# Linear attention on one core: outer products by pair of heads, the carry's sum on VectorE, half sums in the last turn

## The chip, the core and the metric

The kernel runs on one core of a Trainium2 chip. The metric is the device time of one execution in microseconds (us), the median of several. TensorE (PE) multiplies, VectorE (DVE), ScalarE (ACT) and GpSimd (POOL) work element by element, SyncE (SP) issues DMAs. Each engine takes its instructions in the order in which they are written, and waits on semaphores.

## What is computed

A block of 4 x 1024 tokens of width 128: an expert layer, then chunked linear attention with decay, then the same expert layer once more, each added to the tokens. Only the attention is touched here:

```python
def step(kv, xs):                       # 8 chunks of 128 tokens
    qi, ki, vi = xs                     # 4 batches, 16 heads of 8
    scores = einsum('bhid,bhjd->bhij', qi, ki) * mask
    o = einsum('bhij,bhjd->bhid', scores, vi)
    o = o + lam_q[:, :, None] * einsum('bhid,bhde->bhie', qi, kv)
    kv = lam_c[:, None, None] * kv + einsum('bhid,bhie->bhde', ki * lam_k[:, :, None], vi)
    return kv, o
# q, k, v = silu(x @ Wq), silu(x @ Wk), silu(x @ Wv), split into heads
# then a layer norm of o, times sigmoid(x @ Wg1 @ Wg2), @ Wo, added to x
```

## The kernel before

It has three stages: expert layer 0 (to about 147 us of the span), attention in eight turns, one per chunk of all four batches (147 to 307 us), then routing and expert layer 1. The attention kernel does not form the scores. For each token it forms the outer product of k and v of each head (8 x 8 numbers, 64 per head, 1024 per token and batch), multiplies these with a decay matrix over the 128 tokens of the chunk (a matmul per head: the running state at each token), multiplies by q, and sums over d. What comes from earlier chunks goes by a carry, a block-diagonal 128 x 128 matrix per batch.

In turn n, for pairs of heads h = 0 to 7:

- GpSimd forms the outer products (`outer_part`, line L301 through `outer_product`): one instruction makes 512 numbers of one batch and half of the heads; 8 instructions a turn. The four of the first half for turn n + 1 are at the end of turn n, the four of the second half at the start of turn n + 1 around the first half sum. For turn 0 VectorE makes the first half (`first_outer`).
- TensorE forms the state products of pair h (`state_product`, L1287) into bank h % 3. For h = 0 it waits until all four products of the first half are done, for h = 4 for the second half. Between the pairs it does the output product of turn n - 2, the transposes and projections (L1266) of turn n + 1, the gate product; after them the inter product (L1295, needs the carry), the carry product (L1304, needs kd and qdT of turn n + 1), the transposes of o_n (L1184) and the router's product (L1190).
- VectorE multiplies by q (`times_q`, L988, qS with four buffers) and sums over d (`sum_d`, L997, into o_in). For h = 0, 1, 2, 4, 5, 6 of turns 0 to 6, GpSimd first adds the two halves of qS (`half_sum`, L461), and the sum is over 256 numbers in place of 512. Between these stand the small steps of the layer norms, which end in `shift` (L759); `front` makes qdT (L978) behind the steps of pair 6; `join` (L1007), `gate` (L1016), the router's bias (L780) and the statistics (L719) stand at the turn's end and start.
- ScalarE copies xnT, does `age_carry` (L644, L645: the carry times its decay; the new part out of PSUM), then Silu of q, k and v in one instruction per batch (L603, in the first expert layer's end L613), tanh of the gate, and the norms (L544, L636).
- GpSimd also scales the keys (`decay_keys`, L432, kd), masks the new part of the carry and adds it (`update_carry`, L439 and L444), and in turns 0 to 3 fetches the first expert layer's results of the last three chunks back, three indirect DMAs a turn (`fetch_one`, L404), each chunk followed by an add (`add_back`, L411).

After turn 7 VectorE routes the tokens of the first five chunks (L818 to L906), GpSimd gathers them, and expert layer 1 starts.

The order on GpSimd is written out by hand in its `attention(n)`. `helped(n, h)` says which pairs get a half sum.

## Time and profile before

| | us |
|---|---|
| median of 3 runs | 452.91 |
| lowest, highest | 452.79, 458.83 |
| profiled execution: its time | 454.72 |
| profiled execution: its span, first to last instruction | 452.7 |
| mean granted TensorE clock of the profiled execution | 0.928 |

Busy shares of the span: PE 81%, DVE 65%, POOL 65%, ACT 43%. Half of the instructions of TensorE are weight loads, counted apart (PEld). The span is counted from the first instruction. "Idle before" is the time for which an engine stood still ahead of an instruction, with what ended that; L12 is line 12 of the kernel. A granted clock of 1.00 is the 2.4 GHz level. The records of instructions that follow one another closely overlap by up to some 0.1 us, so back to back a duration counts for a little less.

### The profile page before, as it was taken

How to read it: one execution, taken by the hardware profiler on the slowest of the kernel's cores; microseconds unless marked ns; L12 is line 12 of the kernel's file. 1: busy time of each engine (PE TensorE's matmuls, PEld its weight loads, DVE VectorE, ACT ScalarE, POOL GpSimd, SP SyncE). 2: the span in 40 equal slices, each digit the busy share in tenths (PEclk: the TensorE clock that was granted, in tenths of full speed). 3: DMA queues.
4: the chain of work that ended last, by engine and by line, in shares of the span. 5: the costliest groups of instructions: out<-in, count | busy, mean ns of one | idle time of the engine just before them, and what ended most of it. 6: DMA issues, size and time to landing. Idle time of an engine off the chain costs nothing.

```text
span 452.7 us, 10251 instructions
## 1 busy us (share of the span) xinstructions
PE 364.9 (81%) x2508; PEld 325.6 (72%) x2508; DVE 293.9 (65%) x996; ACT 195.9 (43%) x586; POOL 294.2 (65%) x306
## 2 busy tenths in 40 slices
PE   4966999999988977886859889852388999999930
PEld 4955988999977765765657767732387988999920
DVE  3594567444464886685949898897856677666510
ACT  2552663555545232435344745413065434555500
POOL 0006772763886699989787898910277777777771
PEclk9999999999999999696969999995669999999985
DMA  7736787787861000001010101101278855776510
GB/s 230 268 94 203 226 234 183 217 202 217 222 181 30 20 6 17 4 16 46 20 47 1 47 2 46 46 2 46 74 215 241 202 185 161 219 209 198 159 35 0
DMA packets 41303, 54.00 MB, mean 119 GB/s; under 512 B 6212, under 2 KB 25818, under 8 KB 40992
## 3 DMA queue, kind: packets, MB, share of 16 engines
q1 hardware_dynamic: 34496, 39.49, 27.8%
q0 software_dynamic: 6176, 13.26, 12.2%
q10 hardware_dynamic: 576, 0.62, 0.5%
q8 instruction: 23, 0.38, 0.3%
q14 instruction: 32, 0.26, 0.2%
HBM read 41.93 MB, written 12.32 MB: 120 GB/s over the span
## 4 chain that ended last, share of the span: by engine, by line
PE 48%; POOL 23%; DVE 11%; issue 10%; DMA 3%; DVEq 1%; ACT 1%; POOLq 1%; ACTq 0%
PE bank L1238 15%; PE bank L1228 15%; POOL outer_all L301 9%; PE bank L1287 5%; POOL rows L404 4%; POOL qS L461 4%; PE bank L1190 3%; PE bank L1184 2%; PE bank L1266 2%; PE bank L1220 2%; PE bank L1322 2%; POOL out_x L423 1%; DMA const_sb<-in_const 1%; DVE outer_all L895 1%; POOL rows L411 1%
## 5 line engine op out<-in xcount | busy, mean ns | idle before, releaser
L390 POOL DMA_INDIRECT ring<-rows_d,token_in x92 | 88.1, 957 | 98.2 <-DVE token_in L906 71.4
L1228 PE MATMUL bank<-slot_xT,w_ring 128*128 128x128 f32 x736 | 104.7, 285 | 5.3 <-DVE hT_b L946 4.4
L1228 PEld LDWEIGHTS bank<-slot_xT,w_ring 128*128 128x128 f32 x736 | 94.6, 199 | 8.5 <-DVE hT_b L946 6.2
L1287 PE MATMUL bank<-outer_all,decay_sb 128*128 128x256 f32 x256 | 69.5, 397 | 14.6 <-POOL outer_all L301 12.6
L946 DVE TENSOR_SCALAR hT_b<-bank,b_cur 128x128 f32<-128x128 f32 x184 | 55.9, 345 | 38.5 <-PE bank L1228 32.8
L1287 PEld LDWEIGHTS bank<-outer_all,decay_sb 128*128 128x128 f32 x256 | 48.5, 198 | 32.0 <-POOL outer_all L301 13.8
L1238 PE MATMUL bank<-w_sb,hT_a 128*128 x368 | 60.6, 288 | 3.7 <-issue 0.9
L301 POOL TENSOR_TENSOR outer_all<-qkv 128x512 f32<-128x512 f32 x60 | 62.6, 1069 | 1.5 <-ACT qkv L613 1.4
L575 ACT ACTIVATE hT_a<-bank,b_cur 128x128 f32<-128x128 f32 x184 | 57.5, 364 | 12.9 <-PE bank L1228 12.4
L1238 PE MATMUL bank<-w_sb,hT_b 128*128 x368 | 56.8, 277 | 0.0
L423 POOL DMA_INDIRECT out_x<-ring,token_out x46 | 46.7, 1014 | 14.0 <-issue 12.5
L1238 PEld LDWEIGHTS bank<-w_sb,hT_a 128*128 128x128 f32 x368 | 49.4, 195 | 8.8 <-issue 8.3
L997 DVE TENSOR_REDUCE o_in<-qS 128x64 f32<-128x256 f32 (+1 forms) x64 | 47.8, 758 | 12.1 <-POOL qS L461 11.7
L988 DVE TENSOR_TENSOR qS<-bank,qkv 128x512 f32<-128x512 f32 x64 | 43.9, 686 | 17.6 <-PE bank L1287 17.4
L568 ACT ACTIVATE b_cur<-b_t 128x4 f32 x92 | 18.8, 205 | 82.0 <-DVE hT_b L946 62.2
L1238 PEld LDWEIGHTS bank<-w_sb,hT_b 128*128 128x128 f32 x368 | 49.3, 195 | 0.0
L461 POOL TENSOR_TENSOR qS<-qS 128x256 f32<-128x256 f32 x42 | 30.5, 728 | 18.1 <-DVE qS L988 17.9
L404 POOL DMA_INDIRECT rows<-y_d,slot_of x32 | 30.7, 960 | 14.0 <-DMA y_d<-y_sb 6.9
L560 ACT ACTIVATE slot_xT<-bank 128x128 f32<-128x128 f32 x92 | 25.0, 272 | 19.0 <-PE bank L1220 15.4
L1220 PE MATMUL bank<-const_sb,ring 128*128 128x128 f32 x92 | 26.3, 286 | 5.3 <-DMA ring<-rows_d,token_in 2.7
L938 DVE TENSOR_TENSOR ring<-ring,b_sb 128x128 f32<-128x128 f32 x46 | 13.4, 292 | 21.4 <-issue 17.4
L719 DVE BATCH_NORM_STATS2 st<-rows 128x6 f32<-128x128 f32 x96 | 20.7, 279 | 8.8 <-DMA rows<-in_x 7.5
(130 smaller groups left out, 528.3 us busy)
## 6 DMA issues: line engine op xcount, KB each, us to landing
w_ring<-in_w1t SPq DMA_DIRECT2D x92, 256.0 KB
rows_d<-rows SPq DMA_DIRECT2D x8, 512.0 KB, 2.9
y_d<-y_sb SPq DMA_DIRECT2D x46, 64.0 KB
rows<-in_x SPq DMA_DIRECT2D x8, 256.0 KB, 7.5
w_sb<-in_w2t SPq DMA_DIRECT2D x1, 2048.0 KB, 8.6
rows_d<-rows SPq DMA_DIRECT2D x8, 256.0 KB, 2.8
ring<-rows_d,token_in POOLq DMA_INDIRECT x92
decay_sb<-in_decay SPq DMA_DIRECT2D x1, 1024.0 KB, 7.5
```

The source lines that it names most:

```text
L301: return eng.tensor_tensor(u_.rearrange("p (h d e) -> p h d e", d=HD, e=HD), k_.rearrange("p (h d) e -> p h d e", d=HD), v_, ALU.mult)
L390: pool.indirect_dma_start(n_in_ring(G) if layer_of(G) == 0 else in_ring(G), None, rows_d[u], bass.IndirectOffsetOnAxis(ap=token_in[u][:, j ...
L404: pool.indirect_dma_start(n_of(t), None, y_d[u], bass.IndirectOffsetOnAxis(ap=slot_of[u][:, t - UNIT[u].first:t - UNIT[u].first + 1], axis ...
L423: pool.indirect_dma_start(out, bass.IndirectOffsetOnAxis(ap=token_out[u - GROUPS][:, at:at + 1], axis=0), x_in_ring(G), None, bounds_check ...
L461: pool.tensor_tensor(v[:, :, 0], v[:, :, 0], v[:, :, 1], ALU.add).then_inc(halved, 1)
L575: last = nc.scalar.activation(hT_a[G % 2][:, f * P:(f + 1) * P], bank_a[:, f * P:(f + 1) * P], ACT.Relu, bias=b1_cur[G % 2][:, f:f + 1])
L946: last = nc.vector.tensor_scalar(hT_b[G % 2][:, f * P:(f + 1) * P], bank_b[:, f * P:(f + 1) * P], b1_cur[G % 2][:, 2 + f:3 + f], 0.0, ALU. ...
L988: nc.vector.tensor_tensor(qS[h % 4][:, :].rearrange("p (b a e) -> p b a e", b=BATCH, e=HD), bank[h % 3][:, :].rearrange("p (b a e) -> p b ...
L997: nc.vector.tensor_reduce(o_in[:, h * w:(h + 1) * w].rearrange("p (a e) -> p a e", e=HD), qS[h % 4][:, :].rearrange("p (a d e) -> p a e d" ...
L1228: last = mm(to[:, f * P:(f + 1) * P], w1_ring[G % W1_BUFS][:, (2 * half + f) * P:(2 * half + f + 1) * P], slot_xT[G % 2][:, :], start=True ...
L1238: last = mm(y_bank[l][:, 0:D], h[:, f % 2 * P:(f % 2 + 1) * P], w2_sb[:, bass.ds(expert[G] + f * D, D)], start=(f == 0), stop=(f == FB - 1))
L1287: last = mm(to, decay_sb[:, (2 * h + a) * P:(2 * h + a + 1) * P], u, start=True, stop=True)
```

## The change

- q, k and v have another layout in SBUF: q of all batches first, then k and v by head, then batch, then element. Silu becomes two instructions per batch, one for k and v (256 columns, written in runs of 8), one for q.
- One outer-product instruction makes one pair of heads for all four batches (512 numbers again), and all are GpSimd's, turn 0's too. State product h waits for h + 1 of them. In GpSimd's order five (pairs 0 to 4) stand at the end of the turn before, three (5 to 7) at the start of the turn. Pair 0's stands before half sum 6 in turns without an `add_back`.
- The carry is kept unmasked: VectorE computes carry_all = carry_all x decay + new part, straight from PSUM, at the turn's start before `times_q(0)`; GpSimd masks it into carry with one instruction, once the last inter product has read it. `age_carry` goes from ScalarE.
- The 12 fetches are spread as 2, 3, 3, 2, 2 over turns 0 to 4, and `add_back` stands after half sum 5 of turns 1, 3 and 4.
- Half sums: pairs 0, 1, 2, 4, 5, 6 as before in turns 0 to 6, and now pairs 0 to 6 of turn 7.

The diff, without declarations:

```diff
-        helped = lambda n, h: n < STEPS - 1 and h % 4 != 3
+        helped = lambda n, h: h < PAIRS - 1 and (n == STEPS - 1 or h != 3)
+        kv_by_head = lambda par: qkv[par][:, BATCH * D:].rearrange("p (c b e) -> p c b e", b=BATCH, e=HD)
+        k_of, v_of = (lambda par, i=i: kv_by_head(par)[:, i * HEADS:(i + 1) * HEADS] for i in range(2))
+        q_of = lambda par, b: qkv[par][:, b * D:(b + 1) * D]
+        PW = 2 * BATCH * UH
+        BACK_IN_TURN = (2, 3, 3, 2, 2)
+        ADDED_IN_TURN = {1: SPLIT[0][0], 3: SPLIT[0][0] + 1, 4: SPLIT[0][0] + 2}
...
 # GpSimd
-                pool.tensor_tensor(per_batch(kd[n % 2][:, :]),
-                                   qkv[n % 2][:, :].rearrange("p (b w) -> p b w", b=BATCH)[:, :, D:2 * D],
-                                   cst("decay_k").unsqueeze(1).to_broadcast([P, BATCH, D]), ALU.mult).then_inc(kd_done, 1)
-
-            def update_carry(n):
-
-                pool.wait_ge(delta_copied, n + 1)
-                pool.tensor_tensor(per_batch(carry_new[:, :]), per_batch(carry_new[:, :]),
+                pool.tensor_tensor(kd[n % 2][:, :].rearrange("p (b h e) -> p h b e", b=BATCH, e=HD), k_of(n % 2),
+                                   cst("decay_k").rearrange("p (h e) -> p h e", e=HD).unsqueeze(2).to_broadcast([P, HEADS, BATCH, HD]),
+                                   ALU.mult).then_inc(kd_done, 1)
+
+            def mask_carry(n):
+
+                pool.wait_ge(carry_summed, n + 1)
+                pool.wait_ge(inter_ready, n + 1)
+                pool.tensor_tensor(per_batch(carry[:, :]), per_batch(carry_all[:, :]),
                                    cst("carry_mask").unsqueeze(1).to_broadcast([P, BATCH, D]),
-                                   ALU.mult).then_inc(delta_masked, 1)
-                pool.wait_ge(delta_masked, n + 1)
-                pool.wait_ge(carry_aged, n + 1)
-                pool.tensor_tensor(carry[:, :], carry[:, :], carry_new[:, :], ALU.add).then_inc(carry_done, 1)
...
+                pool.wait_ge(qkv_done, BATCH * (n + 1))
                 wait(pool, state_ready, PAIRS * (n - 1))
+                flat = lambda part: part(n % 2)[:, 2 * h:2 * h + 2].rearrange("p h b e -> p (h b) e")
+                k_ = flat(k_of).unsqueeze(3).to_broadcast([P, 2 * BATCH, HD, HD])
+                v_ = flat(v_of).unsqueeze(2).to_broadcast([P, 2 * BATCH, HD, HD])
+                pool.tensor_tensor(outer[n % 2][:, h * PW:(h + 1) * PW].rearrange("p (a d e) -> p a d e", d=HD, e=HD),
+                                   k_, v_, ALU.mult).then_inc(outer_done, 1)
...
             def attention(n):
+                fetches = BACK_IN_TURN[n] if n < len(BACK_IN_TURN) else 0
                 if n > 0:
+                    outer_part(n, 5)
+                    outer_part(n, 6)
                 half_sum(n, 0)
                 if n > 0:
+                    outer_part(n, 7)
+                if fetches > 0:
+                    fetch_one()
                 half_sum(n, 1)
+                if fetches > 1:
+                    fetch_one()
                 half_sum(n, 2)
                 if n + 1 < STEPS:
                     decay_keys(n)
                 half_sum(n, 3)
+                if n > 0:
+                    mask_carry(n - 1)
                 half_sum(n, 4)
+                if fetches > 2:
+                    fetch_one()
                 half_sum(n, 5)
+                if n in ADDED_IN_TURN:
+                    add_back(ADDED_IN_TURN[n])
+                else:
+                    outer_part(n + 1, 0)
                 half_sum(n, 6)
+                for h in range(1 if n not in ADDED_IN_TURN else 0, 5):
+                    outer_part(n + 1, h)
...
+            for h in range(PAIRS):
+                outer_part(0, h)
             for n in range(STEPS):
                 attention(n)
...
 # ScalarE
+            def split_qkv(s, b):
+                act.wait_ge(qkv_ready, BATCH * s.n + b + 1)
+                from_ = bank[3 + b % 2]
+                nc.scalar.activation(kv_by_head(s.par)[:, :, b], from_[:, D:3 * D].rearrange("p (c e) -> p c e", e=HD), ACT.Silu)
+                nc.scalar.activation(q_of(s.par, b), from_[:, 0:D], ACT.Silu).then_inc(qkv_done, 1)
...
-                if s.n >= 2:
-                    age_carry(s.n - 2)
...
 # VectorE
+            def update_carry(n):
+
+                dve.wait_ge(delta_ready, n + 1)
+                dve.wait_ge(carry_cleared, 1)
+                wait(dve, carry_summed, n)
+                wait(dve, carry_done, n + 1)
+                nc.vector.scalar_tensor_tensor(out=carry_all[:, :], in0=carry_all[:, :], scalar=cst("decay_c"), in1=bank[6][:, :],
+                                               op0=ALU.mult, op1=ALU.add).then_inc(carry_summed, 1)
...
                     if 0 <= k - 1:
+                        update_carry(k - 1)
                         last = output_stats(k)
...
-                46: lambda: (first_outer(), front(step(0)))})
+                46: lambda: front(step(0))})
...
 # TensorE
-                if s.n == 0 and h == 0:
-                    pe.wait_ge(first_outer_done, 1)
-                if s.n > 0 or h >= PAIRS // 2:
-                    pe.wait_ge(outer_done, 2 * s.n + h // (PAIRS // 2))
+                pe.wait_ge(outer_done, PAIRS * s.n + h + 1)
...
-                    v_ = qkv[s.par][:, b * 3 * D + 2 * D:(b + 1) * 3 * D]
-                    last = mm(bank[6][:, b * D:(b + 1) * D], kd[s.par][:, b * D:(b + 1) * D], v_, start=True, stop=True)
+                    last = mm(bank[6][:, b * D:(b + 1) * D], kd[s.par][:, b * D:(b + 1) * D], v_of(s.par)[:, :, b],
+                              start=True, stop=True)
```

## Rows read from the trace of the kernel before

**Rows 1.** The view by windows cut by attention turns: length, busy (instructions) per engine, clock, DMA:

```profile
163.80:184.80 21.00, 16.04 (x71) 12.23 (x71) 15.08 (x45) 7.49 (x16) 20.38 (x22) 0.86 0.04 11
...
207.80:233.00 25.20, 19.08 (x91) 15.47 (x91) 16.66 (x51) 10.35 (x22) 20.51 (x22) 0.84 0.12 37
233.00:253.00 20.00, 18.27 (x90) 14.89 (x90) 16.34 (x49) 7.68 (x16) 16.22 (x18) 0.90 0.05 18
253.00:271.10 18.10, 16.44 (x90) 13.27 (x90) 16.66 (x51) 10.15 (x23) 16.15 (x18) 1.00 0.09 31
...
289.20:307.30 18.10, 11.14 (x55) 8.82 (x56) 16.88 (x44) 5.20 (x12) 6.58 (x6) 0.94 0.09 30
```

**Rows 2.** The view of waits, 190 to 330 us: total, times, longest:

```profile
PE bank L1287 <- POOL outer_all L301: 9.8, 5, 4.6
...
POOL qS L461 <- DVE qS L988: 10.9, 12, 1.7
```

**Rows 3.** The timeline of POOL: start, us, line, out<-in, times, idle before:

```profile
165.83 0.73 POOL L461 TENSOR_TENSOR qS<-qS 128x256 f32<-128x256 f32 x1
...
172.55 0.98 POOL L404 DMA_INDIRECT rows<-y_d,slot_of  x1 [0.16 <-issue]
...
176.81 1.26 POOL L444 TENSOR_TENSOR carry<-carry,carry_new 128x512 f32<-128x512 f32 x1
...
181.61 5.16 POOL L301 TENSOR_TENSOR outer_all<-qkv 128x512 f32<-128x512 f32 x5
187.73 0.72 POOL L461 TENSOR_TENSOR qS<-qS 128x256 f32<-128x256 f32 x1 [0.95 <-DVE qS L988]
...
226.88 1.27 POOL L411 TENSOR_TENSOR rows<-rows 128x512 f32<-128x512 f32 x1 [1.68 <-DMA rows<-y_d,slot_of]
```

**Rows 4.** The timeline of PE, at the turns' first products and one carry product:

```profile
184.78 2.08 PE L1287 MATMUL bank<-outer_all,decay_sb 128*128 128x256 f32 x4 [1.62 <-POOL outer_all L301]
...
232.98 2.07 PE L1287 MATMUL bank<-outer_all,decay_sb 128*128 128x256 f32 x4 [4.57 <-POOL outer_all L301]
...
286.41 1.13 PE L1304 MATMUL bank<-qkv,kd 128*128 128x128 f32 x8 [1.28 <-DVE qdT L978]
...
289.22 1.13 PE L1287 MATMUL bank<-outer_all,decay_sb 128*128 128x256 f32 x4 [0.31 <-POOL outer_all L301]
```

**Rows 5.** The timelines of ACT, DVE and POOL around the first turn:

```profile
142.58 0.49 ACT L613 ACTIVATE qkv<-bank 128x384 f32<-128x384 f32 x1 [0.15 <-PE bank L1266]
...
144.68 2.48 DVE L301 TENSOR_TENSOR outer_all<-qkv 128x512 f32<-128x512 f32 x4
...
149.41 0.73 POOL L461 TENSOR_TENSOR qS<-qS 128x256 f32<-128x256 f32 x1 [4.80 <-DVE qS L988]
...
153.15 1.27 POOL L432 TENSOR_TENSOR kd<-qkv,const_sb 128x512 f32<-128x512 f32 x1
```

**Rows 6.** The timeline of DVE in turns 5, 6 and 7:

```profile
256.43 0.69 DVE L988 TENSOR_TENSOR qS<-bank,qkv 128x512 f32<-128x512 f32 x1 [0.91 <-PE bank L1287]
...
277.80 0.59 DVE L997 TENSOR_REDUCE o_in<-qS 128x64 f32<-128x256 f32 x1
...
292.22 0.69 DVE L988 TENSOR_TENSOR qS<-bank,qkv 128x512 f32<-128x512 f32 x1 [1.07 <-PE bank L1287]
292.82 0.68 DVE L1021 SCALAR_TENSOR_TENSOR rows<-bank,rows 128x512 f32<-128x512 f32 x1
...
295.44 1.07 DVE L997 TENSOR_REDUCE o_in<-qS 128x64 f32<-128x512 f32 x1
...
305.11 0.16 DVE L759 SCALAR_TENSOR_TENSOR shift<-bank,rstd 128x8 f32<-128x8 f32 x1
```

**Rows 7.** The groups of ACT by line and shape: times, busy, mean ns, idle:

```profile
L603 ACT ACTIVATE qkv<-bank 128x384 f32<-128x384 f32 x20 | 9.8, 491 | 15.1 <-PE bank L1266 15.1
...
L644 ACT ACTIVATE carry<-carry,const_sb 128x512 f32<-128x512 f32 x6 | 4.3, 712 | 0.0
...
L560 ACT ACTIVATE slot_xT<-bank 128x128 f32<-128x128 f32 x92 | 25.0, 272 | 19.0 <-PE bank L1220 15.4
```

More of the change, by code:

```diff
@@ L291, in build @@
         first_of_unit = lambda G: UNIT[unit_of(G)].start == G
-        def outer_product(eng, n, half, b):
-            w = HEADS // 2
-            at = b * 3 * D + half * w * HD
-            k_ = qkv[n % 2][:, at + D:at + D + w * HD].unsqueeze(2).to_broadcast([P, w * HD, HD])
-            v_ = (qkv[n % 2][:, at + 2 * D:at + 2 * D + w * HD].rearrange("p (h e) -> p h e", e=HD)
-                  .unsqueeze(2).to_broadcast([P, w, HD, HD]))
-            u_ = outer[n % 2][:, b * UW + half * w * UH:b * UW + (half + 1) * w * UH]
-            return eng.tensor_tensor(u_.rearrange("p (h d e) -> p h d e", d=HD, e=HD),
-                                     k_.rearrange("p (h d) e -> p h d e", d=HD), v_, ALU.mult)
+        BACK_IN_TURN = (2, 3, 3, 2, 2)
+        ADDED_IN_TURN = {1: SPLIT[0][0], 3: SPLIT[0][0] + 1, 4: SPLIT[0][0] + 2}
+        assert sum(BACK_IN_TURN) == SPLIT[0][1] * BATCH and len(ADDED_IN_TURN) == SPLIT[0][1]
         block = ctx.enter_context(nc.Block())
@@ L446, in outer_part @@
-            def outer_part(n, half, b):
-                if n == 0 and half == 0 or n == STEPS:
+                pool.tensor_tensor(kd[n % 2][:, :].rearrange("p (b h e) -> p h b e", b=BATCH, e=HD), k_of(n % 2),
[5 more added lines that the diff above has]
+                pool.tensor_tensor(per_batch(carry[:, :]), per_batch(carry_all[:, :]),
+                                   cst("carry_mask").unsqueeze(1).to_broadcast([P, BATCH, D]),
+                                   ALU.mult).then_inc(carry_done, 1)
@@ L516, in _ @@
             add_back(SPLIT[0][0] - 1)
-            for b in range(BATCH):
-                outer_part(0, 1, b)
+            for h in range(PAIRS):
+                outer_part(0, h)
             for n in range(STEPS):
                 attention(n)
-            gather(UNIT[2].start + AHEAD_GATHERS, UNIT[3].start)
+            gather(UNIT[2].start, UNIT[3].start)
             scatter(LAYER_TILES, LAYER_TILES + EARLY_RESULTS)
@@ L601, in attn_front @@
                 for b in range(BATCH):
-                    act.wait_ge(qkv_ready, BATCH * s.n + b + 1)
-                    nc.scalar.activation(qkv[s.par][:, b * 3 * D:(b + 1) * 3 * D], bank[3 + b % 2][:, 0:3 * D],
-                                         ACT.Silu).then_inc(qkv_done, 1)
+                    split_qkv(s, b)
             def copy_first_xn():
@@ L611, in first_qkv @@
                 for b in (first, first + 1):
-                    act.wait_ge(qkv_ready, b + 1)
-                    nc.scalar.activation(qkv[0][:, b * 3 * D:(b + 1) * 3 * D], bank[3 + b % 2][:, 0:3 * D],
-                                         ACT.Silu).then_inc(qkv_done, 1)
+                    split_qkv(step(0), b)
             def gate_tanh(s):
@@ L982, in times_q @@
             def times_q(s, h):
[L984 removed]
                 wait(dve, o_in_done, PAIRS * s.n + h - 3)
                 dve.wait_ge(state_ready, PAIRS * s.n + h + 1)
+                q_ = qkv[s.par][:, 0:BATCH * D].rearrange("p (b w) -> p b w", b=BATCH)
                 q2 = q_[:, :, h * 2 * HD:(h + 1) * 2 * HD].unsqueeze(3).to_broadcast([P, BATCH, 2 * HD, HD])
@@ L1048, in router_bias @@
                 add_router_bias(s * BATCH * EXPERTS, bank[4], BATCH, logits_added)
-            def first_outer():
-                dve.wait_ge(qkv_done, BATCH)
-                for b in range(BATCH):
-                    last = outer_product(nc.vector, 0, 0, b)
-                last.then_inc(first_outer_done, 1)
+            def update_carry(n):
[5 more added lines that the diff above has]
+                                               op0=ALU.mult, op1=ALU.add).then_inc(carry_summed, 1)
             def attention(k):
@@ L1309, in q_transpose @@
                 wait(pe, gate_done, s.n)
-                transpose4(bank[6], lambda b: qkv[s.par][:, b * 3 * D:b * 3 * D + D], qT_ready)
+                transpose4(bank[6], lambda b: q_of(s.par, b), qT_ready)
             def out_transpose(s):
```

68 lines of the change are left out of this document (16 added, 52 removed).

## The prediction

> **What bounds the kernel now.** I read the page first: no engine is busy for more than 81% of the span, and the chain that ended last names GpSimd's product line L301 high up, so a stage in the middle must hang on GpSimd. The view by windows, cut where each attention turn's first state product starts, shows where [rows 1]: turn 1 takes 21.0 us, turn 3 takes 25.2, turn 4 takes 20.0, turn 5 takes 18.1, and turn 7 (no projections, no next turn to prepare) 18.1. GpSimd is busy 20.4 of 21.0 us in turn 1, yet only 16.15 of 18.1 in turn 5. The granted clock is 1.00 in turn 5 and 0.84 to 0.90 in turns 1, 3 and 4.
>
> The waits between 190 and 330 us say who holds whom [rows 2]: TensorE waits 9.8 us for the products of L301, 4.6 us at once, and GpSimd in its turn waits 10.9 us for VectorE's qS.
>
> The reader should next take GpSimd's own timeline of turn 1 [rows 3]. From the first half sum (165.83) to the end of the work before the next turn's first half sum (187.73, less 0.95 idle) are 20.95 us of unbroken work: 8 products of 1.03, 6 half sums of 0.68, three indirect fetches of 1.13 with their gaps, kd, mask, carry add and add_back of about 1.27 each. All four products of the first half of the next turn (181.61, five in one block, of which three belong to it) are the last thing in that queue, and TensorE's first state product needs all four. Then GpSimd has to wait: 0.95 us before a half sum, since TensorE and VectorE start the turn only then; in turn 3 also 1.68 us for a DMA before add_back.
>
> TensorE's timeline [rows 4] shows the other side. The waits for L301 before the first product are 1.62 us (184.78), 4.57 (232.98), 0.31 (289.22). After the long ones four matmul records take 2.07 us, after the short ones 1.13: the granted clock has fallen from its 2.4 GHz level towards 1.2. Turn 4 has no fetches and the same work as turn 5, and takes 1.9 us more; that is what a fallen clock costs a turn that TensorE bounds. With no wait for GpSimd, turn 6 would take 18.1 - 0.3 = 17.8: TensorE works without a break, but for 1.28 us before the carry product (286.41), where it waits for qdT of VectorE.
>
> So: turns 1 to 3 are bound by GpSimd plus a start-up exchange, turn 4 by a fallen clock, turns 5 and 6 by the loop of TensorE, VectorE and ScalarE at 17.8 to 18.1, turn 7 by VectorE.
>
> **The change part by part.**
>
> *Start.* The last two Silu copies of the first qkv start at 142.58 [rows 5]; the split adds some 0.45 us for the last pair of batches (priced below), so all four batches are there at 143.5. GpSimd then does all 8 products of turn 0, 8 x 1.03 = 8.2, until 151.8; before, it did four, and VectorE four in 2.48 us (144.68). Turn 0's first half sum was at 149.41 and comes at 151.8 now. TensorE needs only the first pair, so it starts some 1.1 us earlier, but VectorE's first sum needs the half sum; the gain of the early start is lost there.
>
> *Turn 0 on GpSimd:* 6 half sums 4.1, two fetches 2.3, kd 1.27, five products of the next turn 5.15: 12.8. End of the fifth product of turn 1, E0 = 151.8 + 12.8 = 164.6 (before, end of its four products: 163.7). kd is written in another order, in runs of 8 elements; the products of L301 walk such runs too, at 1.03 us, kd takes 1.27 [rows 5]: I take 1.27 and see at most some 0.2 of gain.
>
> *Carry.* The add L444 (1.27, [rows 3]) leaves GpSimd's queue in each of seven turns. Its turn-1 work becomes 20.95 - 1.3 = 19.65; turn 2 (three fetches, no add_back) 19.65 - 1.25 = 18.4; turns 3 and 4 (two fetches and add_back) 18.5 each; turns 5 and 6, 14.9. ScalarE loses two copies of 512 columns a turn, which lay in front of qkv; I count nothing for them.
>
> *Products by pair.* State product h needs h + 1 products, not half of them. So TensorE starts a turn when it is through with the last, and GpSimd's own order is filled: the idle 0.95 before the first half sum and most of the other waits for qS [rows 2] should go, and add_back no longer follows its fetch at once, so the 1.68 goes. With VectorE in step: in such a turn, counted from the end of GpSimd's fifth product, half sum 0 ends at 2.75, half sum 2 at 7.5, VectorE's sums 2 to 5, qS 5 to 7 and qdT take 5.7 more (three sums of 0.5, one of 1.05, four operations of 0.7, small steps and signals; 13.2), the carry product, out transposes and route product 2.5 [rows 4], and TensorE is at the next turn's first product at 15.8, some 2.7 before GpSimd's fifth product at 18.5. VectorE's sums 6 and 7 (1.5), join and gate (1.3), bias and stats (1.7), carry and first qS (1.3) end at 19.3 with their signals, against half sum 0's start at 20.5. GpSimd need not wait.
> So E1 = 164.6 + 19.65 = 184.2; E2 = 202.6; E3 = 221.1; E4 = 239.6. Turn 5 starts on TensorE 2.6 before E4, at 237.0 (before: 253.0).
> Turns 5 and 6 are the engine loop again: 18.1 each (project waits for ScalarE's xnT, which a smaller wait for GpSimd does not move). Turn 7 starts at 237.0 + 36.2 = 273.2, 16.0 us earlier than 289.22.
>
> *The carry on VectorE.* One scalar_tensor_tensor of 512 from PSUM: L1021 is that form, 0.68, of which 0.60 counts back to back. Seven times 0.6 = 4.2 us on VectorE. It stands before the first qS. The wait for TensorE before the second qS covers it: 0.91 us in turn 5, 1.07 in turn 7 [rows 6]. With that cover gone it costs 0.6 a turn. It waits for the carry product, over long before, and for the mask of the turn before. Behind it queue all qS; I see nothing late. TensorE's inter product waits for the one GpSimd pass instead of two.
>
> *Half sums in the last turn.* A sum over 512 takes 1.07, one over 256 takes 0.59 [rows 6]: 0.49 less each. Six come before the shift (305.11) on which o_n, the route product and the routing hang: 2.9 us. GpSimd has 3 products, 7 half sums and one mask, 9.2 us, in a turn of 15, and each half sum has over a pair's 1.25 us of VectorE work to be done in. The Trainium skill's "GPSIMD Engine Reference", section "Engine selection", speaks against it, and against moving the first products: two-input elementwise work belongs on VectorE, GpSimd being about 2x slower. The rows agree on the size (0.62 against 1.03 for a product), but not that it matters: here the slower engine has the room.
>
> *Split qkv.* One Silu of 384 columns takes 491 ns, a copy of 128 takes 272 [rows 7]. Two instructions of 256 and 128: at least nothing more, at most 0.27 more; I take 0.2, 0.8 a turn, against two copies for the carry that go (L644 takes 712 ns, L645 a little less). ScalarE waits 1.0 us before each, so it is hidden even if writing in runs of 8 costs half as much again. Of matmuls that read v with a stride the trace has no row; state products used to read four blocks of 64 and now one of 256, at least no worse. I take the carry product as it is; from below, no gain, from above see the rival.
>
> **Sum.** 16.0 + 2.9 = 18.9 us off the profiled span of 452.7, giving 433.8. The profiled execution took 454.72, 2.0 outside the span; it is 1.8 above the median of 452.91. Off the median: 434.0. Nothing between turn 7 and the end is changed: routing, gathers and the second expert pass follow one another in a chain that starts with that shift, so they move as they are.
>
> **Rivals.**
> *The clock still falls* (0.18). By my schedule TensorE still idles 2 to 3 us before the carry product in turns 1 to 4. For it: the 1.62 at the end of turn 1 was already followed by slow matmuls (184.78). Against it: 1.28 and 0.31 at the end of turn 6 were not (286.41, 289.22), and my waits lie between [rows 4]. If it falls in each, a turn takes 17.8 + 1.9 = 19.7 in place of 18.4, three times, and 0.1 in turn 1: 438 to 439.
> *The half sums don't help the last turn* (0.07), the rule above as a mechanism: each sum waits for its half sum, which is slower than what it spares. The 2.9 is lost: 437.
> *VectorE becomes the bound* (0.09): it is busy 16.7 us of turn 5, and 17.3 with the carry; if its exchanges with GpSimd leave gaps of 1.5, turns are 18.8, six turns lose 0.4 to 0.7: 437.
> *Strided v slows the carry product* (0.06), the other side. The eight matmuls take 0.94 us in a place where TensorE is the loop, in seven turns. They read v in 16 runs of 8. At 4 times the time (3.8 us) each turn loses 2.8, the whole 18.9; from there the kernel is slower: at 5 times, 460. For it: nothing in the trace; against it: state products read runs of 64 at full pace.
> *It does not shorten the turns* (0.04): GpSimd's turn work falls by 1.3 only, and if its waits come back in other places, 7 x 1.3 = 9 plus 2.9: 441.
>
> **How the numbers follow.** The forecast of 434 has 0.56; its own range is 430 to 438. With the three cases up to 439 that is 0.90; the range 429 to 441 takes in the unfilled gaps and a part of the fifth. About 2% (below 443.9, above 462) is what a measurement of this kernel can tell. Slower: 0.05, 0.04 of it the strided v at over 4 times; within 2%: 0.08, the rest of that case and the upper tails of the others, above all of the fifth; faster: 0.87.
>
> **What would show it.** Right: first state product of turn 7 near 273; turns 1 to 4 at 18.4 to 19.7; no wait of TensorE for L301 over 1 us; GpSimd without idle from 143.5 to about 240; a granted clock of 1.00 in turns 1 to 4; the new carry line 0.68; turn 7 about 15. Wrong: a clock of 0.85 in these turns, carry products over 1.1 us, kd over 1.3, half sums waiting for qS, sums waiting for half sums after turn 4.

## The result and the profile after

| | before | changed |
|---|---|---|
| median, us | 452.85 | 437.02 |
| lowest, highest | 452.65, 458.83 | 435.55, 438.07 |
| profiled execution: time, span | 454.72, 452.7 | 438.07, 436.0 |

The ratio is 0.9617, with a 95% interval of 0.9533 to 0.9702: 3.8% faster. The forecast was 434.0, its range 429 to 441.

The view by windows of the changed kernel, cut at each turn's first state product as in [rows 1] (length, then busy time and instructions of PE, PEld, DVE, ACT, POOL, then the granted clock, DMA share and GB/s; one row a turn from turn 0 on; the last is turn 7 as far as 290):

```profile
147.30:164.80 17.50, 14.35 (x68) 11.32 (x68) 13.43 (x40) 5.05 (x14) 17.16 (x20) 0.92 0.04 12
164.80:182.10 17.30, 16.00 (x73) 12.59 (x72) 14.81 (x44) 5.05 (x14) 16.42 (x18) 0.88 0.04 11
182.10:202.30 20.20, 16.55 (x81) 12.95 (x80) 18.07 (x52) 7.37 (x19) 19.68 (x22) 0.93 0.04 11
202.30:221.30 19.00, 16.94 (x91) 13.30 (x91) 17.13 (x50) 9.98 (x25) 17.72 (x20) 0.98 0.11 36
221.30:239.50 18.20, 16.51 (x93) 13.15 (x92) 17.26 (x51) 9.40 (x25) 17.86 (x19) 1.00 0.11 37
239.50:257.70 18.20, 16.50 (x93) 13.14 (x92) 17.21 (x51) 9.40 (x25) 17.67 (x20) 1.00 0.09 30
257.70:275.90 18.20, 16.52 (x93) 13.15 (x92) 16.52 (x47) 9.41 (x25) 15.00 (x17) 1.00 0.09 29
275.90:290.00 14.10, 10.50 (x55) 8.48 (x55) 13.85 (x45) 3.69 (x10) 8.57 (x11) 1.00 0.12 39
```

Turns 1, 3 and 4, 21.0, 25.2 and 20.0 us in [rows 1], take 17.3, 19.0 and 18.2; turn 5 takes 18.2, where it took 18.1. GpSimd is busy for 16.4 of 17.3 and 19.7 of 20.2 us in turns 1 and 2. The clock is no longer below 0.88, but not 1.00 everywhere.

TensorE's timeline of the changed kernel (start, us, line, out<-in, times, idle before): where it still waits, and what it does behind the wait. Line L1281 is the carry product, L1263 the state product, L1217 the first expert layer's end:

```profile
146.88 0.61 PE L1217 MATMUL bank<-w_sb,hT_b 128*128 x4
147.33 1.03 PE L1263 MATMUL bank<-outer_all,decay_sb 128*128 128x256 f32 x4
...
163.01 2.04 PE L1281 MATMUL bank<-qkv,kd 128*128 128x128 f32 x8 [3.15 <-DVE qdT L954]
164.85 1.91 PE L1263 MATMUL bank<-outer_all,decay_sb 128*128 128x256 f32 x4
...
180.53 1.13 PE L1281 MATMUL bank<-qkv,kd 128*128 128x128 f32 x8 [1.29 <-DVE qdT L954]
...
199.60 2.03 PE L1281 MATMUL bank<-qkv,kd 128*128 128x128 f32 x8 [2.85 <-DVE qdT L954]
...
218.97 1.13 PE L1281 MATMUL bank<-qkv,kd 128*128 128x128 f32 x8 [1.30 <-DVE qdT L954]
221.32 1.11 PE L1263 MATMUL bank<-outer_all,decay_sb 128*128 128x256 f32 x4
```

No first state product waits for GpSimd's products any more; in [rows 4] that was up to 4.57 us. What is left are waits for qdT before the carry product, 3.15 us in turn 0 and 2.85 in turn 2. Behind both, eight records of 128 columns take 2.04 us, in place of 1.13: the granted clock fell there.

GpSimd's timeline, at the points where it starts, waits, or ends a turn's work (L451 is the outer product):

```profile
144.55 8.25 POOL L451 TENSOR_TENSOR outer_all<-qkv 128x512 f32<-128x512 f32 x8 [4.23 <-ACT qkv L580]
...
161.49 6.18 POOL L451 TENSOR_TENSOR outer_all<-qkv 128x512 f32<-128x512 f32 x6
168.03 0.72 POOL L459 TENSOR_TENSOR qS<-qS 128x256 f32<-128x256 f32 x1 [0.35 <-DVE qS L964]
...
180.40 7.22 POOL L451 TENSOR_TENSOR outer_all<-qkv 128x512 f32<-128x512 f32 x7
...
199.74 6.19 POOL L451 TENSOR_TENSOR outer_all<-qkv 128x512 f32<-128x512 f32 x6
206.88 0.72 POOL L459 TENSOR_TENSOR qS<-qS 128x256 f32<-128x256 f32 x1 [0.94 <-DVE qS L964]
...
218.06 7.21 POOL L451 TENSOR_TENSOR outer_all<-qkv 128x512 f32<-128x512 f32 x7
...
236.43 7.22 POOL L451 TENSOR_TENSOR outer_all<-qkv 128x512 f32<-128x512 f32 x7
```

From 144.55 to 242 us it waits for VectorE twice, 0.35 us (168.03) and 0.94 us (206.88). In the kernel before, such waits came to 9.4 us between the first half sum and the end of turn 4 (the 10.9 of [rows 2] is for 190 to 330 us).

### The profile page after: what moved, and what is told of

Its sections match the earlier page's. It is cut to its first block, busy times and chain, and to the rows that moved or that the text cites. A ratio compares the mean times of both kernels' runs of the same rounds, so it can differ in the third digit from the quotient of the medians.

```text
span 436.0 us, 10283 instructions
## 1 busy us (share of the span) xinstructions
PE 359.2 (82%) x2508; PEld 321.0 (74%) x2508; DVE 292.4 (67%) x999; ACT 189.3 (43%) x604; POOL 294.1 (67%) x311
## 4 chain that ended last, share of the span: by engine, by line
PE 54%; DVE 15%; POOL 11%; issue 9%; DMA 3%; ACT 3%; DVEq 1%; POOLq 0%; ACTq 0%
PE bank L1217 16%; PE bank L1207 15%; PE bank L1263 7%; PE bank L1245 4%; PE bank L1163 4%; POOL rows L402 3%; POOL outer_all L451 3%; PE bank L1169 2%; PE bank L1281 2%; POOL qS L459 2%; PE bank L1199 2%; DVE st L695 2%; DMA const_sb<-in_const 2%; POOL out_x L421 2%; DVE outer_all L871 1%
## 5 line engine op out<-in xcount | busy, mean ns | idle before, releaser
L922 DVE TENSOR_SCALAR hT_b<-bank,b_cur 128x128 f32<-128x128 f32 x184 | 56.0, 346 | 38.9 <-PE bank L1207 32.2
L451 POOL TENSOR_TENSOR outer_all<-qkv 128x512 f32<-128x512 f32 x64 | 66.4, 1064 | 4.2 <-ACT qkv L580 4.2
L1263 PE MATMUL bank<-outer_all,decay_sb 128*128 128x256 f32 x256 | 67.7, 390 | 0.8 <-DVE qS L964 0.8
L1217 PE MATMUL bank<-w_sb,hT_a 128*128 x368 | 60.7, 288 | 3.9 <-issue 1.0
L1263 PEld LDWEIGHTS bank<-outer_all,decay_sb 128*128 128x128 f32 x256 | 48.2, 197 | 16.1 <-issue 4.9
L1217 PE MATMUL bank<-w_sb,hT_b 128*128 x368 | 56.8, 278 | 0.0
L1217 PEld LDWEIGHTS bank<-w_sb,hT_a 128*128 128x128 f32 x368 | 49.4, 195 | 9.3 <-issue 8.6
L421 POOL DMA_INDIRECT out_x<-ring,token_out x46 | 46.7, 1016 | 14.0 <-issue 11.9
L1217 PEld LDWEIGHTS bank<-w_sb,hT_b 128*128 128x128 f32 x368 | 49.2, 195 | 0.0
L973 DVE TENSOR_REDUCE o_in<-qS 128x64 f32<-128x256 f32 x64 | 44.4, 704 | 4.3 <-POOL qS L459 4.3
L459 POOL TENSOR_TENSOR qS<-qS 128x256 f32<-128x256 f32 x49 | 35.5, 727 | 8.7 <-DVE qS L964 8.5
L914 DVE TENSOR_TENSOR ring<-ring,b_sb 128x128 f32<-128x128 f32 x46 | 13.5, 293 | 21.8 <-issue 17.8
L1245 PE MATMUL bank<-wqkv_sb,xnT 128*128 128x384 f32 x64 | 26.2, 496 | 1.6 <-DVE qS L964 0.8
```

What stands on the lines that cost most here:

```text
L421: pool.indirect_dma_start(out, bass.IndirectOffsetOnAxis(ap=token_out[u - GROUPS][:, at:at + 1], axis=0), x_in_ring(G), None, bounds_check ...
L451: pool.tensor_tensor(outer[n % 2][:, h * PW:(h + 1) * PW].rearrange("p (a d e) -> p a d e", d=HD, e=HD), k_, v_, ALU.mult).then_inc(outer_ ...
L459: pool.tensor_tensor(v[:, :, 0], v[:, :, 0], v[:, :, 1], ALU.add).then_inc(halved, 1)
L922: last = nc.vector.tensor_scalar(hT_b[G % 2][:, f * P:(f + 1) * P], bank_b[:, f * P:(f + 1) * P], b1_cur[G % 2][:, 2 + f:3 + f], 0.0, ALU. ...
L973: nc.vector.tensor_reduce(o_in[:, h * w:(h + 1) * w].rearrange("p (a e) -> p a e", e=HD), qS[h % 4][:, :].rearrange("p (a d e) -> p a e d" ...
L1217: last = mm(y_bank[l][:, 0:D], h[:, f % 2 * P:(f % 2 + 1) * P], w2_sb[:, bass.ds(expert[G] + f * D, D)], start=(f == 0), stop=(f == FB - 1))
```

## The experiments

Two kinds of numbers are used. The median of four executions moves by 1 to 2 us from run to run, and in the profiled executions a good part lies ahead of the changed stage: the first expert layer ends between 143.6 and 147.3 us. So beside the median stands the length of the stage in the profiled execution, from the moment TensorE is through with the first expert layer to the first gather of the second. It is the gather's start less turn 0's first state product, plus what TensorE waited ahead of that product. Before: 324.25 - 147.31 + 1.15 = 178.1. Changed: 307.49 - 147.33 = 160.2, and 160.2 once more in a second profile. The difference is 17.9 us.

The stage comes from one profile of each kernel, two of the changed one, and it has a spread of its own. Turns 0 to 4 have the same instructions in the changed kernel and in e2, and take 92.2, 91.7 and 91.0 us from turn 0's first product to turn 5's. From turn 7's first product to the first gather the same instructions take 31.6 us in some profiles and 32.2 in others. So a difference of about 1 us in the stage shows nothing by itself.

| kernel | edit | median | stage | against the changed kernel |
|---|---|---|---|---|
| before | | 452.9 to 454.7 | 178.1 | +17.9 |
| changed | | 437.0; 436.3 | 160.2; 160.2 | |
| e1 | coarse waits | 441.6 | 165.5 | +5.3 |
| e2 | no half sums in turn 7 | 438.6 | 162.5 | +2.3 |
| e3 | four first products on VectorE | 436.6 | 159.8 | -0.4 |
| e5 | before, carry alone | 449.2 | 172.4 | (before -5.7) |
| e6 | before, half sums alone | 450.6 | 174.5 | (before -3.6) |
| e7 | one more pass on GpSimd | 441.7 | 166.2 | +6.0 |
| e8 | carry behind the first two qS | 437.6 | 161.6 | +1.4 |
| e9 | before, fetches alone | 452.4 | 178.3 | (before +0.2) |
| e10 | turn 0 in the others' order | 437.8 | 160.9 | +0.7 |
| e11 | no half sum 0 in turns 0 to 4 | 434.7 | 158.7 | -1.5 |
| e12 | e10 and e11 | 432.4 | 157.0 | -3.2 |

The kernel before ran beside each of the three groups, with medians of 453.42 (e1 to e4), 454.4 (e5 to e8) and 454.68 (e9 to e12).

e4 is the changed kernel once more, in the group of e1 to e3 (436.3 in the table); the stage it left was 160.2.

> The changed kernel itself, for comparison on the same chip in the same job: 435.5 to 438, median near 437.

### What GpSimd's queue is worth: e7

```diff
+                pool.tensor_tensor(per_batch(spare_carry[:, :]), per_batch(carry_all[:, :]),
+                                   cst("carry_mask").unsqueeze(1).to_broadcast([P, BATCH, D]), ALU.mult)
                 pool.tensor_tensor(per_batch(carry[:, :]), per_batch(carry_all[:, :]),
```

> The changed kernel with the carry's mask done twice on GpSimd (once into a spare tile): 1.27 us more in its queue in each of turns 1 to 7. Theory (GpSimd bounds turns 1 to 4, the loop of TensorE, ScalarE and VectorE turns 5 and 6, VectorE turn 7): the first products of turns 2 to 5 come 1.3 us later each, 5.1 in all, turns 5 to 7 take what they took; time 442. Rival (GpSimd bounds no turn any more): 438 or less.

Median 441.7, stage 166.2. The view by windows of e7, turns 1 to 5:

```profile
161.60:181.50 19.90, 15.35 (x72) 12.06 (x71) 15.82 (x46) 5.05 (x14) 19.03 (x21) 0.87 0.04 10
181.50:201.90 20.40, 16.91 (x80) 13.03 (x79) 17.09 (x51) 7.37 (x19) 19.87 (x22) 0.92 0.04 11
201.90:222.40 20.50, 18.26 (x93) 14.40 (x91) 18.15 (x52) 10.73 (x27) 19.61 (x21) 0.92 0.10 34
222.40:242.20 19.80, 18.50 (x91) 15.33 (x91) 16.71 (x51) 8.71 (x23) 18.92 (x21) 0.87 0.11 34
242.20:260.40 18.20, 16.50 (x92) 13.14 (x91) 17.20 (x51) 9.40 (x25) 17.79 (x19) 1.00 0.09 30
```

Turn 5's first product comes 97.3 us after turn 0's, where it comes after 92.2 and 91.7 us in the two profiles of the changed kernel: 5.1 to 5.7 us more, for 4 x 1.27 = 5.1 us of added work. Turn 5 takes 18.2 in both, though it has the added work too. The theory is right: GpSimd sets the time of turns 1 to 4, and the engine loop sets turn 5. The rest of the 6.0 in the stage lies behind turn 7's first product, where the first gather comes after 32.5 us (31.6 and 32.2 in the changed kernel).

### What the wait by pair is worth: e1

```diff
-                pe.wait_ge(outer_done, PAIRS * s.n + h + 1)
+                pe.wait_ge(outer_done, PAIRS * s.n + (5 if h < 5 else PAIRS))
```

> The changed kernel with the wait of the state products made coarse again: pairs 0 to 4 wait for all five products that stand at the turn's end, pairs 5 to 7 for all eight. No instruction is added or taken away. Theory (starting each turn on the first pair is what earns most of the 16 us): the first state product waits for GpSimd's fifth product again, in turns 1 to 4 VectorE and GpSimd exchange at the start (about 1 us idle before half sum 0, some more before half sum 2), the granted clock falls behind the waits, a turn takes 2 to 3 us more; time 445 to 449. Rival (the add that left GpSimd's queue and the spread of the fetches earn it): 437 to 440.

Median 441.6, 5.3 above the changed kernel in the same group (436.3), ratio 0.9751 (0.9719 to 0.9784) to before. It lies between the two expectations. TensorE's timeline of e1 at the first products of turns 0 to 4:

```profile
147.99 1.49 PE L1263 MATMUL bank<-outer_all,decay_sb 128*128 128x256 f32 x4 [2.37 <-POOL outer_all L451]
...
165.60 2.08 PE L1263 MATMUL bank<-outer_all,decay_sb 128*128 128x256 f32 x4 [1.06 <-POOL outer_all L451]
...
186.15 2.07 PE L1263 MATMUL bank<-outer_all,decay_sb 128*128 128x256 f32 x4 [3.36 <-POOL outer_all L451]
...
206.00 1.13 PE L1263 MATMUL bank<-outer_all,decay_sb 128*128 128x256 f32 x4 [1.59 <-POOL outer_all L451]
...
225.24 1.13 PE L1263 MATMUL bank<-outer_all,decay_sb 128*128 128x256 f32 x4 [1.55 <-POOL outer_all L451]
```

The waits for GpSimd's last product are back, 2.37, 1.06, 3.36, 1.59 and 1.55 us. But only behind those of turns 1 and 2 (165.60, 186.15) are the products slow throughout; in turns 3 and 4 they take 1.13, as at full clock. Turns 1 to 4 take 20.6, 19.9, 19.2 and 18.6 us, where the changed kernel has 17.2, 20.2, 19.0 and 18.2: it is turn 1 that gets longer, and ahead of turn 0 stand the 2.37 us. Turn 5's first product comes 6.0 us later, counted from the end of the first expert layer, and two things make up 5.7 of it. GpSimd waits 4.9 us for VectorE's qS up to there, in place of 1.3; and TensorE no longer starts turn 5 2.1 us ahead of GpSimd's fifth product. Turn 5 is 0.6 us shorter. So starting on the first pair earns 5.3 us, a third of the 15.8 by which the median fell, and not most of them.

### What each part earns alone: e5, e6, e9, e2

e5 puts the diff's `update_carry` and `mask_carry` into the kernel before and takes `age_carry` and the add out of it; nothing else.

> The kernel before, with only the carry's part of the change: VectorE sums it out of PSUM unmasked, GpSimd masks it in one pass, ScalarE's two copies go. Layout, coarse waits, fetches and half sums stay as before. Theory: 1.3 us leave GpSimd's queue in turns 1 to 3, which it bounds, and nothing is gained in turns 4 to 6; turn 7 nothing; VectorE's 0.6 is covered; time 448 to 450. Rival (the carry is the main part): 442 or less. Rival (VectorE's added 0.6 at the turn's start delays the first half sum, which is on the path): 452 or more.

Median 449.2 against 454.4 in its group (ratio 0.9878, 0.985 to 0.9906), stage 5.7 shorter. The view by windows of e5, turns 1 to 4:

```profile
163.20:183.60 20.40, 16.14 (x71) 12.19 (x71) 15.84 (x47) 7.12 (x15) 19.12 (x21) 0.92 0.04 11
183.60:204.80 21.20, 16.78 (x78) 13.31 (x78) 16.89 (x51) 7.70 (x17) 19.06 (x21) 0.91 0.03 9
204.80:227.40 22.60, 17.81 (x90) 14.42 (x90) 17.16 (x52) 10.22 (x23) 19.16 (x21) 0.93 0.10 33
227.40:246.60 19.20, 17.87 (x91) 14.88 (x91) 16.45 (x50) 6.07 (x12) 15.72 (x17) 0.91 0.08 28
```

GpSimd is busy 19.1 us in each of turns 1 to 3, 1.3 less than in [rows 1]. Turn 1 gets 0.6 us shorter, turn 2 1.8 and turn 3 2.6. Of turn 3's 2.6, 1.3 is the work, and 1.1 a wait of GpSimd for a qS, 1.51 us before (216.96) and 0.42 in e5, in a turn whose clock is 0.93 in place of 0.84. Turn 4, where nothing was expected, gets 0.9 shorter. The time came as expected, and both rivals fall; the turns did not share it as expected.

e6 changes one line of the kernel before:

```diff
-        helped = lambda n, h: n < STEPS - 1 and h % 4 != 3
+        helped = lambda n, h: h < PAIRS - 1 and (n == STEPS - 1 or h != 3)
```

> The kernel before, with only the half sums of turn 7 added (pairs 0 to 6). Theory: 2.9 to 3.4 us less, 449.5 to 450. GpSimd still has eight products, two carry passes in that turn and the last of its products at the turn's start, so a rival is that half sums 0 and 1 come late and 1 us of it is lost: 451.

Median 450.6 against 454.4 (ratio 0.9923, 0.9897 to 0.9949), between the expectation and its rival. The first gather comes 32.1 us after turn 7's first product, where it was 35.0: 2.9 less. The other 0.6 of the stage's 3.6 lies in turns that the edit leaves alone. GpSimd had the room for the half sums. e2 takes it out of the changed kernel again:

> The changed kernel without half sums in turn 7. Theory: VectorE bounds turn 7, six sums before the shift take 1.07 in place of 0.59 us, the route product and the routing come 2.9 us later; time 439.9 to 440.5. Rival (each sum waits for its half sum, so nothing is earned): 437.

Median 438.6 against 436.3, 2.3 more, which is below the expected 439.9. The first gather comes 35.1 us after turn 7's first product, 2.9 to 3.5 us later than in the changed kernel. The stage grows by 2.3 only, since turns 0 to 4, where nothing is changed, took 91.0 us in this profile in place of 92.2: turn 0 took 16.6, and none of the waits of turns 0 and 1 was followed by a fallen clock.

e9 spreads the fetches and add_backs of the kernel before as the change does:

> The kernel before, with only the fetches and add_backs spread as in the change (2, 3, 3, 2, 2; added in turns 1, 3, 4). The carry's part alone shortened the stage from turn 0's first state product to the first gather by 5.6 us (176.9 to 171.3), the half sums alone by 3.5, and the coarse waits gave 3.0 of the change's 16.7 back; 4.6 are left. Theory: they are the fetches' (in turns 2 and 3 some 1.2 us of GpSimd work each goes to turn 4, which had room, and the 1.68 us DMA wait goes): stage 172.3 to 173.5, time 449 to 450. Rival (turn 4 pays for what it gets): stage 175 or more.

Median 452.4 against 454.7 (ratio 0.9947, 0.9906 to 0.9989), and the stage is not shorter, 178.3. (The expectation counts from the first product; the 3.0 it names for e1 is 5.3 when TensorE's wait ahead of turn 0 is counted too, and what is left is then 3.3.) The view by windows of e9, turns 3 to 5:

```profile
204.00:226.70 22.70, 19.42 (x91) 15.70 (x91) 16.68 (x51) 10.08 (x22) 19.46 (x21) 0.87 0.10 30
226.70:248.10 21.40, 18.27 (x90) 14.61 (x90) 16.60 (x51) 10.64 (x24) 19.38 (x21) 0.90 0.10 31
248.10:269.20 21.10, 19.32 (x90) 15.75 (x90) 16.45 (x50) 8.80 (x19) 16.19 (x18) 0.85 0.08 26
```

Turn 3 falls from 25.2 to 22.7 us, and turns 4 and 5 take 21.4 and 21.1, where [rows 1] has 20.0 and 18.1. Turn 4 has 19.4 us of GpSimd work now, and turn 5, with work for 16.2, starts at a fallen clock. The rival holds for this profile: the spread earns nothing in the stage, and 3.0 us of what turns 2 and 3 gave went to turn 5 with its clock of 0.85, which may differ in another execution. The medians are 2.2 us apart. In the profiled execution 2.1 us lie ahead of the stage (the first expert layer ends at 144.1, at 146.2 before); whether they do in the others, no profile shows.

Added up, the carry, the half sums and the fetches alone make 5.7 + 3.6 - 0.2 = 9.1 us. All of the change but the wait by pair makes 178.1 - 165.5 = 12.6. The other 3.5 are more than the spread of single profiles, and come only when the parts stand together; whether the layout with its products by pair, their order, or the fetches on top of the carry's part earn them was not separated.

### GpSimd's start in turn 0: e3 and e10

e3 gives the products of pairs 0 to 3 of turn 0 to VectorE:

```diff
+            def first_outer():
+                dve.wait_ge(qkv_done, BATCH)
+                for h in range(FIRST):
+                    pair_product(nc.vector, 0, h).then_inc(first_outer_done, 1)
...
-            for h in range(PAIRS):
+            for h in range(FIRST, PAIRS):
                 outer_part(0, h)
```

> The changed kernel with the products of pairs 0 to 3 of turn 0 on VectorE (in the end of the first expert layer), 4 to 7 on GpSimd as before. Theory (GpSimd is without idle from the first product to the end of turn 4, so what leaves its queue ahead of turn 0 comes off the time): 4 x 1.03 = 4.1 us leave it, less about 1 us because qS 0 is not there earlier: first half sum near 149.5 instead of 152.75, turn 0 without the 3.15 us wait of TensorE before its carry product and without the fallen clock there; time 433.5 to 434.5. Rival (TensorE's own loop of 17.8 to 18.2 a turn takes over at once): 436 or more.

Median 436.6 against 436.3: nothing gained. VectorE's timeline of e3:

```profile
145.64 4.73 DVE L302 TENSOR_TENSOR outer_all<-qkv 128x512 f32<-128x512 f32 x4
```

GpSimd's timeline of e3:

```profile
144.17 5.04 POOL L302 TENSOR_TENSOR outer_all<-qkv 128x512 f32<-128x512 f32 x4 [4.59 <-ACT qkv L584]
152.61 0.73 POOL L463 TENSOR_TENSOR qS<-qS 128x256 f32<-128x256 f32 x1 [3.40 <-DVE qS L970]
```

VectorE's four products took 4.73 us, and they took 2.48 before [rows 5]; GpSimd's four took 5.04, and eight take 8.25 in the changed kernel, 4.12 for four. In the kernel before, GpSimd's had ended at 144.60, and VectorE's began at 144.68; here both ran at once, and each slowed the other. The new layout is not the cause: with both engines at it, one product took up to 1.55 us on VectorE and 1.52 on GpSimd, and VectorE's last, when GpSimd's were through (149.21), took 0.68, as long as in the kernel before. qS 0 came at 151.86 only, and half sum 0 at 152.61, as in the changed kernel (152.75). So GpSimd's queue was not given its start 3 us earlier, and the run says nothing on what that would bring, nor on the rival, though its median lies in the rival's range; the 4.1 us that left the queue became a wait of 3.40. The Trainium skill's "GPSIMD Engine Reference", section "Specifications", says that the two engines share SBUF interfaces and contend when VectorE reads two SBUF inputs; these products do, and the trace agrees.

e10 changes only the order in turn 0: five products, half sum 0, pair 5, a fetch, half sum 1, pairs 6 and 7.

> The changed kernel with turn 0's products in the order of the other turns: pairs 0 to 4, half sum 0, pair 5, a fetch, half sum 1, pairs 6 and 7, and so on. GpSimd has the same work in all. Theory (from its first product to turn 4 GpSimd's total is what counts): half sum 0 comes 3 us earlier, TensorE's 3.15 us wait in turn 0 and the fallen clock behind it go, turn 0 takes 16.5 instead of 17.5, and turn 1 gives it back: stage from turn 0's first state product to the first gather 159.5 to 160.3, like the changed kernel's 160.2. Rival (VectorE and TensorE are the ones that were late): stage 159 or less.

Median 437.8, stage 160.9, 0.6 above the range. TensorE's timeline of e10 at the end of turn 0:

```profile
159.34 1.13 PE L1286 MATMUL bank<-qkv,kd 128*128 128x128 f32 x8 [3.17 <-DVE qdT L959]
```

Half sum 0 comes 3.1 us earlier, but the wait did not go: 3.17 us, where it was 3.15. In turn 0 VectorE needs the half sums one after another, and half sum 2 comes 12.0 us after GpSimd's first product, where it came after 11.9; all eight products and both fetches stand ahead of it in either order. Turn 0 is 0.9 us shorter because the clock did not fall behind the wait, as it did not in e2 and e7, which have the changed kernel's order in turn 0, and the later turns take it back. The order earns nothing; the forecast of an equal stage holds, and the step that was to lead there does not.

### VectorE's share: e8, e11, e12

e8 moves `update_carry(k - 1)` behind `times_q(here, 1)`.

> The changed kernel with VectorE's sum of the carry moved behind the first two qS of the turn, instead of ahead of the output statistics and the first qS. Theory (the 0.65 us lies beside a wait for TensorE in turns 3 to 7; only in turns 1 and 3 did half sum 0 wait for qS, 0.35 and 0.94 us): 0.5 to 1 less than the changed kernel, 436 to 436.5. Rival (VectorE is on the path in every turn): 0.6 x 7 = 4 less, 433.

Median 437.6, stage 161.6, 1.4 longer, and both expectations fall. VectorE's timeline of e8 at the start of turn 3:

```profile
201.81 0.69 DVE L992 SCALAR_TENSOR_TENSOR o_gT<-gateT,bank 128x512 f32<-128x512 f32 x1 [1.07 <-ACT bank L614]
...
203.97 0.67 DVE L964 TENSOR_TENSOR qS<-bank,qkv 128x512 f32<-128x512 f32 x1
205.86 0.69 DVE L964 TENSOR_TENSOR qS<-bank,qkv 128x512 f32<-128x512 f32 x1 [1.21 <-PE bank L1264]
206.46 0.74 DVE L1032 SCALAR_TENSOR_TENSOR carry_all<-carry_all,const_sb,bank 128x512 f32<-128x512 f32 x1
```

and that of the changed kernel:

```profile
203.31 0.69 DVE L992 SCALAR_TENSOR_TENSOR o_gT<-gateT,bank 128x512 f32<-128x512 f32 x1 [1.05 <-ACT bank L614]
...
204.69 0.73 DVE L1032 SCALAR_TENSOR_TENSOR carry_all<-carry_all,const_sb,bank 128x512 f32<-128x512 f32 x1
...
206.12 1.27 DVE L964 TENSOR_TENSOR qS<-bank,qkv 128x512 f32<-128x512 f32 x2
```

In the changed kernel the second qS follows without a wait, in e8 it waits 1.21 us, and the sum stands behind that wait. In the turns that GpSimd bounds this costs next to nothing: turn 5's first product comes 92.4 us after turn 0's, against 91.0 to 92.2, and turns 5 and 6 take 18.2 in both. It shows in turn 7, which VectorE bounds. The shift, on which the routing hangs, comes 13.71 us after turn 7's first product, and 13.07 in the changed kernel, later by the sum's 0.65. There the cover that the prediction named is real. The rest of the 1.4 is no more than the profiles' spread.

e11 leaves half sum 0 out of turns 0 to 4:

```diff
-        helped = lambda n, h: h < PAIRS - 1 and (n == STEPS - 1 or h != 3)
+        helped = lambda n, h: h < PAIRS - 1 and (n == STEPS - 1 or h != 3) and not (n < 5 and h == 0)
```

> The changed kernel without half sum 0 in turns 0 to 4: 0.68 us less on GpSimd and 0.49 us more on VectorE in each. Theory (GpSimd bounds turns 0 to 4, with VectorE close behind it): the stage gets 2 to 3.5 us shorter, 156.7 to 158.2. Rival (VectorE bounds them): 1 to 2.5 us longer, 161 to 162.7. Rival (TensorE's loop of 18.2 takes over): within 1 us of 160.2.

Median 434.7, stage 158.7, 1.5 shorter, less than expected. GpSimd lost 3.4 us of work and its waits at the start of turns 1 and 3, but VectorE is busy 18.4 of turn 2's 19.7 us; that it is the next bound is argued from this, and no run shows it. e12 is e11 and e10 together:

> Both together: turn 0's products in the order of the other turns, and no half sum 0 in turns 0 to 4. Theory: 0.5 to 1.5 us better than the better of the two alone, since GpSimd's chain is shorter and TensorE no longer stalls in turn 0: stage 156 to 157.5, time 433 to 434. Rival (VectorE bounds): 160 or more.

Median 432.4, ratio 0.9499 (0.9423 to 0.9574) to before; stage 157.0. It beats both kernels, the one before by 22 us and the changed one, which ran in other groups, by about 4. Both numbers lie where the theory had them or below, but not by its steps: in turn 0 TensorE still waits 2.45 us for qdT, as in e11, and half sum 2 comes 11.3 us after GpSimd's first product in both. TensorE's timeline at the carry product of turn 2, of e11:

```profile
196.57 2.05 PE L1281 MATMUL bank<-qkv,kd 128*128 128x128 f32 x8 [2.63 <-DVE qdT L954]
```

and of e12:

```profile
196.38 1.13 PE L1286 MATMUL bank<-qkv,kd 128*128 128x128 f32 x8 [2.76 <-DVE qdT L959]
```

e11 waited 2.63 us and then ran at a fallen clock, and its turn 2 took 19.7 us; e12 waited 2.76 and stayed at full clock, 18.6 us. So about 1 us of e12's 1.7 over e11 is a clock that did not fall, and may be there in one execution and not in another; 0.5 more is the stretch from turn 7's first product to the first gather (31.7 against 32.2), where the two have the same instructions. That the order adds anything to e11 is not shown.

## Why the prediction was right, and where it was off

Counted from the end of the first expert layer (146.16 before, 147.33 after), the prediction's steps and what the profile shows:

| | forecast | measured |
|---|---|---|
| end of GpSimd's fifth product, turn 1 (E0) | 18.4 | 18.3 |
| E1 | 38.0 | 38.2 |
| E2 | 56.4 | 56.6 |
| E3 | 74.9 | 75.9 |
| E4 | 93.4 | 94.3 |
| first product of turn 5 | 90.8 | 92.2 |
| first product of turn 7 | 127.0 | 128.5 |
| first gather | 159.2 | 160.2 |

- **GpSimd's chain** was right in mechanism and size: the steps were to be 19.65, 18.4, 18.5 and 18.5, and are 19.9, 18.3, 19.3 and 18.4. e7 shows that it is this queue that counts.
- **"GpSimd need not wait"** failed in turn 3, by the 0.94 at 206.88. Gate waits 1.05 us (203.31 above) for a copy of ScalarE's, which hangs on the output transposes behind the slow carry product of turn 2. Where the clock did not fall the wait is not there. The same carry product in e4 and in e2, with the same instructions up to it:

```profile
198.36 1.49 PE L1281 MATMUL bank<-qkv,kd 128*128 128x128 f32 x8 [2.85 <-DVE qdT L954]
```

```profile
196.53 1.13 PE L1281 MATMUL bank<-qkv,kd 128*128 128x128 f32 x8 [2.79 <-DVE qdT L954]
```

  At 2.03 us (changed kernel), 1.49 (e4) and 1.13 (e2) for this product, gate waits 1.05, 0.51 and 0 us, and GpSimd 0.94, 0.41 and 0. So in turn 3 the working was right for a clock at 1.00, and the step that was off is the clock. The 0.35 in turn 1 is there in all three.
- **TensorE's lead** at turn 5 over GpSimd's fifth product was to be 2.6 us, and is 2.1; 0.5 of the rest.
- **The clock** did not stay at 1.00 in turns 1 to 4 (0.88, 0.93, 0.98, 1.00). The schedule had waits of 2 to 3 us before the carry product in each of turns 1 to 4; only turn 2's is so long (2.85), the others are 1.3. Turn 0's, which the prediction does not name, is 3.15. Behind these two the clock fell. The rival had priced a turn with it at 19.7, 1.9 above 17.8, read from turn 4 of the kernel before. Turn 0 shows less: 17.5 us with the fallen clock, and 16.65 without it in e2 and e7, with the same instructions. Even that is mostly hidden by GpSimd's queue: turns 0 and 1 together take 34.7 and 34.3 us in the changed kernel's two profiles, and 34.3 in e2. Behind turn 2 it costs the 0.94. I had 0.18 on the rival, and my sum carried nothing for it.
- **The last turn**: the term was right. The shift stands 13.07 us after turn 7's first product (275.85), and 15.89 before (305.11 in [rows 6], 289.22 in [rows 4]), 2.8 less for the 2.9 that I took:

```profile
288.92 0.16 DVE L735 SCALAR_TENSOR_TENSOR shift<-bank,rstd 128x8 f32<-128x8 f32 x1
```

  No sum of turn 7 waits for a half sum. The first gather comes 3.4 us earlier against that product in this profile and 2.8 in e4. The 0.6 lies behind the shift, in code that the change leaves alone; that it made up for a part of the 1.5 us by which turn 7 came late is luck.
- **The carry on VectorE**: L1032 takes 0.73 us in place of 0.68, and was covered in turn 7 (e8).
- **Split Silu, kd, strided v**: the two instructions take 0.38 and 0.27 us, kd 1.28, and eight records of the carry product 1.13 at full clock, as in [rows 4]. None costs anything that shows, and the rival on the slower side was empty. ScalarE's waits before the old Silu were 0.8 us each, not the 1.0 that I read (15.1 us for 20 in [rows 7]).
- **Which part earns what** I would have told wrongly: the prediction sums the whole chain, and does not price its parts one by one. My theory for e1 gave the wait by pair 8 to 12 us (445 to 449, for 437); it is 5.3. The spread of the fetches, 1.2 us a turn in that chain and 1.68 of DMA wait, brings the stage nothing alone.
- **From stage to time**: in the stage 1.0 us is missing of 18.9. The first expert layer ended 1.17 us later in the profiled execution than before, in code that hardly differs, and ends between 143.6 and 147.0 in the others; that is the other half of the 2.2 between the forecast span of 433.8 and 436.0. The last 0.8 is the way from profile to median: I took 1.8 off, as before, and it is 1.05.
